# Graph network kernel: unit messages as a float32r high part and an exact rest, target one-hots as the stationary operand

## What is computed

```python
row, col = src, dst                               # 200000 edges
msg = concatenate((x[row], edge_attr), axis=1)
msg = relu(msg @ W1 + b1)                         # 128 features an edge
sums = segment_sum(msg, col, num_segments=n)      # by target node
agg = sums / maximum(count, 1)[:, None]
out = relu(concatenate((x, agg), axis=1) @ W2 + b2)
```

## Time and profile before

| | |
|---|---|
| median of 3 runs | 3475.75 us (3471.35 to 3476.24) |
| profiled execution, first to last instruction | 3499.7 us |
| TensorE busy, whole span | 2746.7 us, 78% |
| VectorE busy | 1592.3 us, 45% |
| ScalarE busy | 1071.7 us, 31% |
| GpSimd busy | 1876.6 us, 54% |
| message stage, first to last L1069 | 2114.8 to 3451.0 us |

### The profile page before, as it was taken

One profiled execution on the slowest core, in us unless ns is written; L12 is line 12 of the kernel. 1 busy time (PEld: TensorE's weight loads), 2 busy tenths in 40 slices (PEclk: granted clock), 3 DMA queues, 4 the chain that ended last, 5 costly groups with the idle time before them and its releaser, 6 DMA issues.

```text
span 3499.7 us, 54147 instructions
## 1 busy us (share of the span) xinstructions
PE 2746.7 (78%) x18926; PEld 2159.2 (62%) x18927; DVE 1592.3 (45%) x3094; ACT 1071.7 (31%) x3149; POOL 1876.6 (54%) x1751
## 2 busy tenths in 40 slices
PE   2755697889947765787878647998998989888987
PEld 0114486777736654565656536777777777777766
DVE  7988985766623433000000253444444444444436
ACT  6504234556625533000000012333333333333321
POOL 3750767778866732534445134565565555555660
PEclk9995989999968977878888768999999999999989
DMA  9012122323322323433434232323233233332321
GB/s 358 28 35 76 34 83 96 130 98 128 147 85 94 133 97 97 159 124 132 163 125 163 91 98 69 94 90 101 90 95 92 86 104 92 89 92 88 105 73 45
DMA packets 127284, 365.86 MB, mean 105 GB/s; under 512 B 36226, under 2 KB 79591, under 8 KB 120599
## 3 DMA queue, kind: packets, MB, share of 16 engines
q10 hardware_dynamic: 21792, 186.56, 13.8%
q0 software_dynamic: 58928, 89.45, 10.0%
q1 hardware_dynamic: 46377, 87.47, 7.1%
HBM read 230.80 MB, written 132.55 MB: 104 GB/s over the span
## 4 chain that ended last, share of the span: by engine, by line
PE 62%; DVE 11%; issue 10%; another core or an unknown queue 8%; ACT 3%; POOL 2%; DMA 1%; ACTq 1%; DVEq 0%; SPq 0%; POOLq 0%
PE ps_feat L920 12%; PE ps_node L920 11%; PE ps_extra L1069 7%; PE ps_sum L1032 4%; PE pre_banks L908 3%; PE pre_banks L1023 3%; PE ps_feat L1057 3%; PE ps_feat L1053 3%; PE ps_sum L1053 2%; PE ps_sum L1057 2%; PE ps_node L1053 2%; PE ps_node L1057 2%; POOL region_b L705 2%; DVE region_c L1757 2%
## 5 line engine op out<-in xcount | busy, mean ns | idle before, releaser
L680 POOL DMA_INDIRECT permuted<-rows_or_lows,slot_of_edge x768 | 871.7, 1135 | 528.3 <-DVE agg L1766 222.9
L662 POOL DMA_INDIRECT rows<-table,region_a x800 | 786.5, 983 | 685.7 <-issue 210.5
L920 PE MATMUL ps_feat<-region_a,region_b 128*128 128x256 bf16 x3528 | 506.9, 290 | 71.4 <-issue 70.8
L920 PE MATMUL ps_node<-region_a,region_b 128*128 128x256 bf16 x3528 | 513.6, 290 | 60.6 <-issue 57.6
L920 PEld LDWEIGHTS ps_feat<-region_a,region_b 128*128 128x128 bf16 x3528 | 359.3, 103 | 156.5 <-issue 97.4
L920 PEld LDWEIGHTS ps_node<-region_a,region_b 128*128 128x128 bf16 x3528 | 358.2, 103 | 148.7 <-issue 86.9
L1069 PE MATMUL ps_extra<-region_b 128*128 128x128 f32 x2352 | 335.0, 284 | 86.4 <-ACT region_b L1299 48.0
L1069 PEld LDWEIGHTS ps_extra<-region_b 128*128 128x128 f32 x2352 | 302.0, 199 | 92.6 <-issue 72.1
L1757 DVE TENSOR_TENSOR region_c<-iota_key,region_c 128x1568 bf16<-128x1568 f16 (+1 forms) x324 | 353.2, 1090 | 0.0
L1933 DVE TENSOR_TENSOR region_b<-consts,region_a 128x512 f32<-128x512 f32 x336 | 208.2, 620 | 186.9 <-PE ps_extra L1069 97.6
L1928 DVE TENSOR_SCALAR region_b<-rows_or_lows,consts 128x512 f32<-128x512 bf16 x336 | 159.8, 479 | 288.8 <-remote 133.1
(11 more groups left out here) (263 smaller groups left out, 4534.9 us busy)
## 6 DMA issues: line engine op xcount, KB each, us to landing
counts<-region_a ACTq DMA_DIRECT2D x24, 3136.0 KB
region_a<-counts ACTq DMA_DIRECT2D x22, 3136.0 KB
rows_or_lows<-block_lows ACTq DMA_DIRECT2D x72, 448.0 KB
permuted<-region_b SPq DMA_DIRECT2D x25, 833.0 KB
region_a<-permuted SPq DMA_DIRECT2D x24, 833.0 KB
rows_or_lows<-edge_cols_in POOLq DMA_DIRECT2D x24, 544.0 KB
region_a<-attr_t_in SPq DMA_DIRECT2D x50, 256.0 KB
rows<-table,region_a POOLq DMA_INDIRECT x800
```

The lines of the kernel that those rows point to most:

```text
L662: nc.gpsimd.indirect_dma_start(rows[:, s, j * D:(j + 1) * D], None, tables[2], bass.IndirectOffsetOnAxis(ap=message_rows[:, c * TC + j:c * ...
L680: nc.gpsimd.indirect_dma_start(permuted, bass.IndirectOffsetOnAxis(ap=slot_of_edge[:, r * RT + k:r * RT + k + 1], axis=0), edge_rows_of[:, ...
L920: ins = mm(strip_bank(buf), parts[:, h, k], counts[buf][:, h], start=(h == 0 and k == 0), stop=(h == SB - 1 and k == PARTS - 1), skip_grou ...
```

## The change

Before, messages and one-hots are float32, the messages stationary. After:

- ScalarE writes relu of the unit into the first half of `block_msgs`, as float32r (`block_message`). That is the high part.
- VectorE has a new operation, `split`: max(PSUM, 0) minus the high part, written to the second half as float32r. It stands after `source` in each step from 2 on, and it is what `block_sums` waits for.
- `block_sums` has the target one-hot (float32r) stationary, and both parts move as 256 columns. The result is target x (high, rest), for a range in one of two banks (`ps_extra`, `ps_turn`).
- At the end of a range VectorE adds the two halves into `range_rows` (`take_rows`, steps 16 and 2), TensorE transposes it into columns 256 to 383 of `ps_sum[0]` (`turn_rows`, steps 17 and 4), and VectorE adds it to `agg` (`add_rows`, steps 18 and 5). The second range of a pair is so finished in the next pair, and the last one after the loop.
- `turn_lows` goes to steps 8 and 23, ahead of `block_products`, into columns 128 to 255 of `ps_sum[0]`; as that bank is shared, `sums_of` and the transposes wait for each other's readers. `store_lows` moves ahead of `block_message`.
- `range_base` is shifted by one entry, some semaphores are merged, and the buffers are laid out anew in the same place.

The diff, cut to its core:

```diff
-LO_TURNED_AT = (7, DU + 10)
+LO_TURNED_AT = (8, DU + 9)
+TAKEN_AT = (DU + 2, 2)
+ROWS_TURNED_AT = (DU + 3, 4)
+ROWS_ADDED_AT = (DU + 4, 5)
...
+            beside("node_rows", [P, NB * D])
+            source_hot = beside("source_hot", [P, 2, unit_blocks * P])
+            target_hot = beside("target_hot", [P, 2, unit_blocks * P], F32R)
+            block_msgs = [beside("block_msgs_0", [P, unit_blocks, 2, D], F32R)]
+            attr_turned = beside("attr_turned", [P, 2, P])
...
+        range_banks = [ps_extra, ps_turn]
+        turned_lows, turned_rows = ps_sum[0][0:SB, P:2 * P], ps_sum[0][:, 2 * P:3 * P]
...
-                def turn_lows(k, r):
+                def turn_lows(k, r, chunks_summed):
 
                     pe.wait_ge(B["prepared"], k * 2 + r + 1)
                     pe.wait_ge(B["lo_evicted"], k * 2 + r + 1)
-                    mm(ps_turn[0:SB, 0:P], block_lo[r][:, 0:SB], ident_bf[:], start=True, stop=True).then_inc(B["lo_turned"], 1)
+                    pe.wait_ge(e["added"], chunks_summed + SLOTS)
+                    mm(turned_lows, block_lo[r][:, 0:SB], ident_bf[:], start=True, stop=True).then_inc(B["lo_turned"], 1)
+
+                def turn_rows(j, chunks_summed):
+
+                    pe.wait_ge(B["taken"], j + 2)
+                    pe.wait_ge(e["added"], chunks_summed + SLOTS)
+                    nc.tensor.transpose(turned_rows, range_rows[:], ident).then_inc(B["rows_turned"], 1)
...
-                    pe.wait_ge(B["msgs"], k * PAIR_UNITS + u + 3)
+                    pe.wait_ge(B["split"], k * PAIR_UNITS + u + 1)
                     pe.wait_ge(B["target"], k * PAIR_UNITS + u + 1)
                     if u % DU == 0:
-                        pe.wait_ge(B["added"], k * 2 + u // DU + 1)
+                        pe.wait_ge(B["taken"], k * 2 + u // DU + 1)
                     for j in range(n):
-                        last = mm(ps_extra[:, 0:P], block_msgs[u % 2][:, j * D:(j + 1) * D], target_hot[u % 2][:, j * P:(j + 1) * P],
+                        last = mm(range_banks[u // DU][:, 0:2 * D], target_hot[:, u % 2, j * P:(j + 1) * P],
+                                  block_msgs[u % 2][:, j].rearrange("p k d -> p (k d)"),
                                   start=(u % DU == 0 and j == 0), stop=(u % DU == DU - 1 and j == n - 1))
...
+                        summed = k * PAIR_CHUNKS + (u + 1) * chunks // PAIR_STEPS
                         if c is not None:
+                            pe.wait_ge(B["lo_evicted"], k * 2 + (2 + (u > LO_TURNED_AT[0]) + (u > LO_TURNED_AT[1] and not last)))
+                            if u >= ROWS_ADDED_AT[1]:
+                                pe.wait_ge(B["added"], k * 2 + (1 + (u >= ROWS_ADDED_AT[0])))
                             sums_of(k, c)
+                        if u == LO_TURNED_AT[0]:
+                            turn_lows(k, 1, summed)
+                        if u == LO_TURNED_AT[1] and not last:
+                            turn_lows(k + 1, 0, summed)
+                        if u == ROWS_TURNED_AT[1]:
+                            turn_rows(k * 2, summed)
+                        if u == ROWS_TURNED_AT[0]:
+                            turn_rows(k * 2 + 1, summed)
                         if 1 <= u <= PAIR_UNITS:
                             block_products(k, u - 1)
                         if 2 <= u:
                             block_sums(k, u - 2)
-                        if u == LO_TURNED_AT[0]:
-                            turn_lows(k, 1)
-                        if u == LO_TURNED_AT[1] and not last:
-                            turn_lows(k + 1, 0)
-
-                turn_lows(0, 0)
+
+                turn_lows(0, 0, 0)
                 pe.wait_ge(B["msgs"], 2)
                 products_of(0, 0)
                 with pe.Fori(0, PAIRS - 1) as k:
                     pair_of(k, PAIR_CHUNKS, False)
                 pair_of(PAIRS - 1, LAST_CHUNKS, True)
+                turn_rows(RANGES, MESSAGE_CHUNKS)
...
-                    nc.scalar.activation(block_msgs[u % 2][:, 0:n * D], banks[u % 3][:, 0:n * D], ACT.Relu).then_inc(B["msgs"], 1)
+                    nc.scalar.activation(block_msgs[u % 2][:, 0:n, 0], banks[u % 3][:, 0:n * D].rearrange("p (j d) -> p j d", d=D), ACT.Relu
+                                         ).then_inc(B["msgs"], 1)
+                        if u == LO_TURNED_AT[0]:
+                            store_lows(k, 1)
+                        if u == LO_TURNED_AT[1] and not last:
+                            store_lows(k + 1, 0)
...
-                dve.sem_inc(B["added"], 1)
+                dve.wait_ge(G["h2"], NG)
+                v.memset(range_banks[1][:, 0:2 * D], 0.0)
+                dve.drain()
+                dve.sem_inc(B["taken"], 1)
...
-                def add_range(k, r, chunks_added):
-                    base = dve.value_load(range_base[0:1, bass.ds(k * 2 + r, 1)], min_val=0, max_val=NP - P)
-                    dve.wait_ge(B["summed"], k * PAIR_UNITS + ((r + 1) * DU + 2))
-                    dve.wait_ge(e["added"], k * PAIR_CHUNKS + (SLOTS + chunks_added))
+                def take_rows(r, units):
+                    dve.wait_ge(B["summed"], units + 2)
+                    v.tensor_reduce(range_rows[:], range_banks[r][:, 0:2 * D].rearrange("p (k d) -> p d k", k=2), AX.X, ALU.add).then_inc(B["taken"], 1)
+
+                def add_rows(j, chunks_added):
+                    base = dve.value_load(range_base[0:1, bass.ds(j, 1)], min_val=0, max_val=NP - P)
+                    dve.wait_ge(B["rows_turned"], j + 1)
+                    dve.wait_ge(e["added"], chunks_added + SLOTS)
                     w = agg[:, bass.ds(base, P)]
-                    v.tensor_tensor(w, w, ps_extra[:, 0:P], ALU.add).then_inc(B["added"], 1)
+                    v.tensor_tensor(w, w, turned_rows, ALU.add).then_inc(B["added"], 1)
                     dve.drain()
+
+                def split(k, u):
+                    n = unit_tiles(u % DU)[1]
+                    dve.wait_ge(B["msgs"], k * PAIR_UNITS + u + 3)
+                    v.scalar_tensor_tensor(out=block_msgs[u % 2][:, 0:n, 1], in0=banks[u % 3][:, 0:n * D].rearrange("p (j d) -> p j d", d=D),
+                                           scalar=0.0, in1=block_msgs[u % 2][:, 0:n, 0].bitcast(F32), op0=ALU.max, op1=ALU.subtract
...
-                        if u == DU + 2:
-                            add_range(k, 0, added)
+                        if u == TAKEN_AT[1]:
+                            take_rows(1, k * PAIR_UNITS)
+                        if u == TAKEN_AT[0]:
+                            take_rows(0, k * PAIR_UNITS + DU)
+                        if u == ROWS_ADDED_AT[1]:
+                            add_rows(k * 2, k * PAIR_CHUNKS + added)
+                        if u == ROWS_ADDED_AT[0]:
+                            add_rows(k * 2 + 1, k * PAIR_CHUNKS + added)
                         if u < PAIR_UNITS:
                             source(k, u)
+                        if 2 <= u:
+                            split(k, u - 2)
...
-                    add_range(k, 1, added)
+                take_rows(1, RANGES * DU)
+                add_rows(RANGES, MESSAGE_CHUNKS)
```

76 lines of the change are left out of this document (37 added, 39 removed).

## The result

The kernel after takes 3522.2 us (median of 4 runs, 3517.47 to 3524.15) against 3475.99 for the kernel before (4 runs): ratio 1.0118 [1.0076, 1.016]. It is slower by 1.2%, some 40 us (the medians lie 46 us apart); forecast was 101 us faster. That holds where these runs were made. Further down the same two kernels run on another chip, where the sign turns.

A forecast was written before the change was run, and what follows sets the result against it. The prediction took TensorE, 91% busy in a 109.8 us pair, to bound the message stage. Its terms, -131 + 3 + 3 + 2 + 21 + 1 = -101 us, took 3475.75 to 3375 us, range 3338 to 3445.

The forecast's parts named there:

- TensorE bounds this stage.: Message stage: TensorE, busy 99.6 of 109.8 us a pair (91%), sets the pace.
- rival (a): Message stage: the new hand-over through VectorE's rest eats more, about 34 us saved, 3440 us; chance 18%.
- The price of float32r: Range sums on TensorE: 0.112 us a block instead of 0.223, saving 131 us over 1176 blocks.
- (c): Range sums: float32r streams no faster than float32, 0.215 us a block or more, 3497 or 3749 us; chance 6%.
- (d): Range sums: float32r weight load doesn't overlap the matmul before it, 0.213 us a block, 3494 us; chance 2%.
- Transposes that wait behind a chunk: TensorE's range transposes and moved low turns: waits cost nothing in eleven pairs, +3 us in the last.
- The hand-over, +21 us: TensorE's sums: 30 waits each grow by VectorE's 0.7 us rest; nothing if waits vanish, 50 us if doubled.
- VectorE's load: Message stage: VectorE's work rises from 48.2 to about 66 us a pair in the profile, below TensorE, so free.
- The clock: Message stage: granted clock near 0.95; a fall to 0.85 would make the forecast wrong by some 10 us a pair.
- No DMA is added, nothing moves past a queue: Transfers: no DMA added, nothing moved past SP's or GpSimd's queue; no cost counted.
- Rival (e): Whole change doesn't act: saved time returns as wait because another thing paces the pair, 3476 us; chance 2%.

The follow-up runs named there:

- e6: Kernel before with only the first of each chunk's four gathers issued; ratio 0.9331 on a second chip, pair 92.9 us.
- e8: Kernel before with each indirect gather replaced by a plain load of 128 consecutive rows, same bytes; ratio 0.9324, pair 92.9 us.
- e10: Kernel before with an extra wait ahead of each gather, spreading gathers over the steps; ratio 1.0023 on a third chip, pair 93.2 us.
- e4: Kernel after with each of the 1176 range-sum matmuls issued a second time into unused columns; ratio 1.0081, pair 113.1 us.
- e14: Kernel after, unchanged, run on a fourth chip where the kernel before takes 2825.5 us; ratio 0.9782, 2762.46 us, pair 87.7 us.
- e1: Kernel after with the low turn two steps later and the first range's rows turned and added two steps later; ratio 1.0027, pair 110.5 us.
- e2: Kernel after without VectorE's rest operations, the sums waiting for ScalarE's high part; ratio 1.0040, pair 110.2 us.
- e18: Kernel after with the first two low-bit loads for the next pair at step 26 instead of 27; ratio 0.9661, 2730.01 us, pair 84.8 us.
- e3: Kernel after with VectorE's rest written to unused columns, the sums not waiting for it; ratio 1.0091, pair 112.2 us.
- e5: Kernel after with only the first of each chunk's four gathers issued; ratio 0.9134 on a second chip, pair 86.9 us.

## Why the prediction was wrong

Point by point, in its own order:

- **"TensorE bounds this stage." This is the step that failed.** It was read off 91% busy. But TensorE's work at full pace is 92.9 to 93.2 us a pair (e6, e8, e10), and the pair took 109.8; the other 17 us were idle time and a lower clock, and went with the indirect gathers. The trace of the kernel before could have told it. By the distances of starts in its smooth steps a pair's work is 28 transposes at 0.11, 14 units of either size at 0.86 and 0.70 (attributes), 0.89 and 0.67 (source), 0.90 and 0.67 (sums), 16 chunks at 0.84, 8 `products_of` at 1.06 and 2 low turns at 0.17: 91 us. The row for `products_of` is not in the earlier trace rows:

```profile
2865.62 1.14 PE L1023 MATMUL pre_banks<-edge_w,region_a 64*128 64x256 f32 x8
2866.68 1.10 PE L1032 MATMUL ps_sum<-onehot,rows 128*128 128x64 f32 x8
```

  The chain's "another core or an unknown queue", on a program that has one core, was the other sign: 7.4%, 8 us of each pair. I listed it under rival (a) as background to the change's own wait, and not as what sets the pair. Where a pair is set by hand-overs, work taken from TensorE turns into its idle time and a lower clock: that is e4, read backwards.
- **The price of float32r:** 0.112 forecast, 0.119 measured; 1176 blocks save 122 us, not 131. The Trainium skill ("FP8 and Floating Point Precision", TensorE Precision Notes), by whose four passes a block would be 108 ns, is off by 11 ns here. Rivals (c) and (d) fell: neither 0.215 nor 0.213. The rule of the Trainium skill that (d) names stands in the section The mechanism of "TensorE: Matmul & The Clock Gate"; 0.119 us for a block with a load of its own disagrees with it too.
- **Transposes that wait behind a chunk "cost nothing":** L1052 and L1058 waited 37 us in ten pairs. The slack of 0.8 us that covered them assumed that VectorE learns of the sums at once. On a chip without late signals L1052 waits 3.4 us in ten pairs (e14), so there the term was right. e1 prices the low turn and the first range's turn at 2.7 us a pair.
- **The hand-over, +21 us:** over the stretch that the forecast went by, TensorE waited at the sums 30 times before, for 52.9 us, and 69 times after, for 97.1 us: +44, twice the forecast. VectorE's rest is 51.3 us of it. The mechanism was named, and so was this case: "50 us if they double in number". The number of waits was the mis-sized part. e2 prices rest and wait together at 3 us a pair. Without late signals it is nearly nothing: 2.8 us in ten pairs (e18).
- **VectorE's load:** 64.8 us a pair (648.32 / 10), forecast 66. Right. That it is free on a chip without late signals is borne out by e18, where TensorE is busy 98% of the pair. With them it isn't known: e3 keeps the load and is 2.3 us a pair above the kernel before, but keeps some of the waits too.
- **The clock:** named as what would make the forecast wrong by 10 us a pair, if it fell to 0.85. It fell from 0.96 to 0.90, 5.8 us a pair.
- **"No DMA is added, nothing moves past a queue":** true and beside the point. The loads of low bits stayed as they were, and the faster pair ran into them: ScalarE's message of a chunk waits 29.9 us in ten pairs for them in e14, 8.5 in e10, where TensorE has the old work. On a chip without late signals that costs 2.9 us a pair, 32 us in all (e18 against e14). What a faster engine collides with was asked for every added wait, not for the fixed transfers.
- **The chances.** 0.08 for slower went to prices of float32r alone. Rival (e), "another thing paces the pair", had 2% and was the right one; with the two waits on top it ends on the slow side, and no rival was that.

A number near the sum of the prediction, -101 us, does appear: -94 us in e18, on a chip without late signals and with the loads put right. Part of that is luck, for two misses cancel: the sums save 9 us less than forecast, and the hand-over costs some 3 us there instead of 21. Still TensorE's part was sound there, and the bound was wrong for the chip at hand. What makes a chip's signals late was not found.

## What to carry to other kernels

Add up the bottleneck's work of one period at full pace, from start distances, and set it against the period, before believing a busy share: here 91 of 110 us. In a one-core profile "remote" or "another core" over 7 to 13% of the chain was the mark of hand-overs that set the pace; there the change that added a hop cost, and the work that it took away gained nothing, until the source of the delay was gone. A cheap test is e4: issue the work a second time, and see whether the time moves. And when an engine gets faster, look at fixed transfers that are issued one step ahead of their wait.

## What the runs showed of the hardware

- Where GpSimd issued indirect DMAs, signals between the other engines came late on two chips: 6.1 us in the wait shown whole, and ScalarE and VectorE waited up to 8.4 us with no releaser found. It is worth 17 us of a 110 us pair, shown by taking the gathers away on one of the chips (e5 to e8). Plain DMAs issued by the same engine with the same bytes don't do it. On these two chips the kernel before took 3423 and 3483 us, on four others 2824.1 to 2825.5; the waits called "remote" are absent in all ten profiles from the latter, though GpSimd issues the same indirect DMAs.
- A pause of 2.4 us on TensorE was followed by products at half pace: 8 matmuls in 1.94 us instead of 1.00, at a granted clock of 0.50 (e14). Moving one pair of loads gave back 16 us of pause and 14 us of slow work.
- One float32r matmul of 256 columns with a load of its own takes 0.119 us in a row, where two float32 instructions of 128 columns take 0.223.
